# Two turns of a gather ring per iteration of VectorE's loop, in seven passes over the edges of a graph

## The chip, the cores and the metric

The kernel runs on one core of one Trainium2 chip. The metric is the device time of one execution, in microseconds. Three executions of the kernel before took 12166.11, 12187.51 and 12193.12 us; their median is 12187.51 us. Less is better.

## The reference

Four graph networks follow one another on one graph with 6250 nodes of 256 features and 100000 edges, sorted by destination. All of them gather the row of an edge's source node and sum such rows by destination node:

```python
# L0 (two layers) and L3: attention. ex is the softmax weight of an edge and head
out = segment_sum(h[src] * alpha[:, :, None], dst, N)
# L1: three graph convolutions
agg = segment_sum(x[src], dst, N); h = elu(agg @ W_rel + b + x @ W_root)
# L2: batch norm network
agg = segment_sum(edge_weight[:, None] * x[src], dst, N)
```

After each network a residual is added and a layer norm taken. So there are seven passes over the edges: two of L0, three of L1, one of L2, one of L3.

## The kernel before

The edges are padded so that every chunk of 128 edges belongs to one tile of 128 destination nodes. There are NCH = 832 chunks. Eight chunks (U = 8) make a unit; a pass has 104 units. The gathered rows lie in a ring with four slots (SLOTS = 4), one unit per slot, so that the ring goes round 26 times in a pass. Four units are called a turn here.

`aggregate_phase` (line 687) is one such pass, called seven times: l0a, l0b and l3 with a weight for each head, l2a with one weight per edge, and l1a, l1b, l1c (called the convolution passes below) with none. In it five instruction streams run beside each other and meet at semaphores only:

- GpSimd (POOL) waits until the index of the next unit is ready and issues eight indirect DMAs (`Ring.gather`, line 681), each of which gathers 128 rows of 1 KB from DRAM into the slot.
- VectorE (DVE) does three things for each unit. `begin` (line 745) builds the member matrices, 128x1024, one instruction for eight chunks (line 750). `take` (line 753) waits for the eight gathers and scales the slot, 128x2048 (line 761 or 765); in the convolution passes it only passes on a semaphore (line 757). `add` (line 768) loads the eight accumulator offsets of the unit into registers (line 772) and adds eight sums out of PSUM into the accumulator (line 779), each after a wait for its matmul (line 777) and one for the add before it.
- TensorE (PE) multiplies the member matrix of a chunk by its rows (line 815). It waits for `begin` and `take` of the unit, and, before it writes over a PSUM bank, for the add of the chunk eight back.
- ScalarE (ACT) waits until TensorE has summed all of a slot and copies the index of the unit four further on (line 731), which frees the slot for GpSimd.

VectorE's stream is written so that `begin` and `take` of the next unit stand ahead of `add` of this one. The loop at line 791 has one turn in its body, four units written out, and runs 25 times (`units // SLOTS - 1`). The 26th turn is written out behind it (lines 797 to 803), since its last unit has no next one. In the loop the unit's number is worked out from the loop's register, and each add has one register instruction for its address (line 776) and one for its wait (line 779); in the written-out turn the numbers are constants.

Of the kernel before, what the change touches and what calls it, by code (L numbers as in the profile page):

```python
# [14 lines left out]
SP_, SC = 125, 800  # L15
U = 8
SLOTS = 4
BY_GATHER = 2
FAR = 2.0 ** 100
NCH = -(-(E // P + 1 + NT) // (U * SLOTS)) * U * SLOTS  # L20
EP = NCH * P
# [19 lines left out]
I32 = mybir.dt.int32  # L41
assert E == SP_ * SC and NCH % (U * SLOTS) == 0 and NCH * P >= E + NT * (P - 1)


class Steps:


    def __init__(self, eng, sem):
        self.eng, self.sem, self.n = eng, sem, 0
# [620 lines left out]
class Ring:  # L670


    def __init__(self, m):
        self.messages = m.sb("messages", [P, SLOTS, U, MSGW])
        self.index = m.sb("index", [P, SLOTS, U], I32)
        self.gathered = [m.sem(f"gathered{s}") for s in range(SLOTS)]

# [9 lines left out]
def aggregate_phase(nc, k, name, table, acc, scale, head_scale, softmax, width, started=None):  # L687

    with ExitStack() as ctx:
        m = Mem(nc, ctx, name)
        slots = started or Ring(m)
        ring, index, gathered = slots.messages, slots.index, slots.gathered
        member = m.sb("member", [P, 2, U, P])
        sums = [m.ps(f"sums{j}", [P, 512]) for j in range(U)]
        turn = m.sem("gather_turn")
        index_ready = m.sem("index_ready")
        set_up = m.sem("set_up")
        prepared = m.sem("prepared")  # L700
        member_made = m.sem("member_made")
        chunk_summed = m.sem("chunk_summed")
        chunk_added = m.sem("chunk_added")
        half_cleared = m.sem("half_cleared")
        block = ctx.enter_context(nc.Block())
        half = NTP * MSGW // 2
        assert head_scale == (started is not None)
        units = NCH // U

        @block.gpsimd  # L710
        def _(pool):
            if started:
                pool.memset(acc[:, half:], 0.0).then_inc(half_cleared, 1)
            with pool.Fori(1 if started else 0, units // SLOTS) as i:
                for s in range(SLOTS):
                    pool.wait_ge(index_ready, i * SLOTS + s + 1)
                    pool.sem_inc(turn, 1)
                    slots.gather(pool, table, s)

        @block.scalar  # L720
        def _(act):
            def fill(s, u, index_too):

                if softmax:
                    ins = act.copy(ring[:, s, :, MSG_P:MSG_P + H],
                                   by_chunk(k.numer)[:, bass.ds(u * U, U), :])
                if width > MSG_M:
                    ins = act.copy(ring[:, s, :, MSG_M:MSG_M + H],
                                   by_chunk(k.first_max)[:, bass.ds(u * U, U), :])
                if index_too:  # L730
                    ins = act.copy(index[:, s, :], k.src[:, bass.ds(u * U, U)])
                ins.then_inc(index_ready, 1)

            act.wait_ge(set_up, 1)
            for s in range(SLOTS):
                fill(s, s, not started)
            with act.Fori(1, units // SLOTS) as i:
                for s in range(SLOTS):

                    act.wait_ge(chunk_summed, i * (SLOTS * U) + (s + 1 - SLOTS) * U)  # L740
                    fill(s, i * SLOTS + s, True)

        @block.vector
        def _(dve):
            def begin(i, s):

                u = i * SLOTS + s
                dve.wait_ge(index_ready, u + 1)

                dve.tensor_tensor(member[:, s % 2], repeat_outer(k.iota[:], U),  # L750
                                  repeat_inner(k.local[:, bass.ds(u * U, U)], P), ALU.is_equal).then_inc(member_made, 1)

            def take(i, s):
                dve.wait_ge(gathered[s], i * (16 * U) + 16 * U)
                msgs = ring[:, s, :, 0:D]
                if scale is None:
                    dve.sem_inc(prepared, 1)
                elif head_scale:
                    heads = msgs.rearrange("p j (h f) -> p j h f", h=H)
                    weights = by_chunk(scale)[:, bass.ds((i * SLOTS + s) * U, U), :]  # L760
                    dve.tensor_tensor(heads, heads, weights.unsqueeze(3).to_broadcast([P, U, H, C]),
                                      ALU.mult).then_inc(prepared, 1)
                else:
                    u = i * SLOTS + s
                    dve.tensor_tensor(msgs, msgs, repeat_inner(scale[:, bass.ds(u * U, U)], D),
                                      ALU.mult).then_inc(prepared, 1)

            def add(i, s):


                u = i * SLOTS + s
                offs = nc.values_load_multi_w_load_instructions(
                    k.tile_off[0:1, bass.ds(u * U, U)], engines=(mybir.EngineType.DVE,),
                    min_val=0, max_val=(NT - 1) * MSGW, skip_runtime_bounds_check_because="made so")[1]
                for j in range(U):
                    dve.wait_ge(chunk_summed, u * U + (j + 1))
                    dve.wait_ge(chunk_added, u * U + (j + 1))
                    at = acc[:, bass.ds(offs[j], width)]
                    dve.tensor_tensor(at, at, sums[j][:, 0:width], ALU.add).then_inc(chunk_added, 1)  # L779

            dve.memset(ring[:, :, :, MSG_ONE], 1.0).then_inc(set_up, 1)
            begin(0, 0)
            if started:

                take(0, 0)
                dve.memset(acc[:, 0:half], 0.0).then_inc(chunk_added, 1)
                dve.wait_ge(half_cleared, 1)
            else:
                dve.memset(acc, 0.0).then_inc(chunk_added, 1)
                take(0, 0)  # L790
            with dve.Fori(0, units // SLOTS - 1) as i:
                for s in range(SLOTS):
                    following = (i + (s + 1) // SLOTS, (s + 1) % SLOTS)
                    begin(*following)
                    take(*following)
                    add(i, s)
            last = units // SLOTS - 1
            for s in range(SLOTS):
                following = (last, s + 1) if s + 1 < SLOTS else None
                if following:  # L800
                    begin(*following)
                    take(*following)
                add(last, s)

        @block.tensor
        def _(pe):
            def sum_unit(i, s, first):
                u = i * SLOTS + s
                pe.wait_ge(member_made, u + 1)
                pe.wait_ge(prepared, u + 1)  # L810
                for j in range(U):
                    if not first:

                        pe.wait_ge(chunk_added, u * U + (j + 2 - U))
                    pe.matmul(sums[j][:, 0:width], member[:, s % 2, j, :], ring[:, s, j, 0:width],  # L815
                              start=True, stop=True).then_inc(chunk_summed, 1)

            for s in range(SLOTS):
                sum_unit(0, s, s == 0)
            with pe.Fori(1, units // SLOTS) as i:  # L820
                for s in range(SLOTS):
                    sum_unit(i, s, False)
# [102 lines left out]
def lookup_phase(nc, k, name, codes_dram, att_dram, z, z_self):  # L925
# [7 lines left out]
    NS = H * NT  # L933
    LP = U - BY_GATHER
    with ExitStack() as ctx:
# [8 lines left out]
        src_member = m.sb("src_member", [P, 2, 2, LP * P], BF16)  # L944
        index = m.sb("index", [P, SLOTS, BY_GATHER], I32)
        rows = m.sb("rows", [P, SLOTS, BY_GATHER, 2 * H])
        picked = m.sb("picked", [P, 2, LP, H])
# [32 lines left out]
        def _(act):  # L980
            def fill(s, u):
                act.copy(index[:, s, :], k.att_row[:, bass.ds(u * U + LP, BY_GATHER)]).then_inc(index_ready, 1)

# [8 lines left out]
        def _(pool):  # L992
            pool.wait_ge(att_stored, 16)
            with pool.Fori(0, units // SLOTS) as i:
                for s in range(SLOTS):
                    pool.wait_ge(index_ready, i * SLOTS + s + 1)
                    pool.sem_inc(turn, 1)
                    for j in range(BY_GATHER):
                        pool.indirect_dma_start(
# [5 lines left out]
        def _(dve):  # L1005
# [22 lines left out]
            def pick(i, r):  # L1028
# [9 lines left out]
                if z_self is not None:  # L1038
                    zs = by_chunk(z_self)[:, bass.ds(u * U, U), :]
                    dve.tensor_tensor(zs, dst[:, :, 0:H], dst[:, :, H:], ALU.add)  # L1040
                dve.wait_ge(gathered[r], i * (16 * BY_GATHER) + 16 * BY_GATHER)
                dve.tensor_tensor(by_chunk(z)[:, bass.ds(u * U + LP, BY_GATHER), :], rows[:, r, :, 0:H],
# [887 lines left out]
```

## Time and profile before

| what | value |
|---|---|
| executions, us | 12166.11, 12187.51, 12193.12 |
| the profiled execution, us | 12139.19 |
| its span, first to last instruction, us | 12137.7 |
| busy PE / PEld / DVE / ACT / POOL, us | 6937.7 / 4270.1 / 6291.8 / 691.5 / 7475.9 |
| mean granted TensorE clock | 0.678 |
| instructions in the profile | 120576 |

The page's busy times are sums over the whole span. No engine is busy for more than 62% of it (POOL), since the seven passes and the phases between them have different limits. The chain that the page follows back from the last instruction covers only the last layer norm and says nothing of the passes. So the passes are read one by one, by windows in time.

### The profile page before, as it was taken

To read this page: it belongs to the slowest core of one execution; us is meant where nothing else is said; L and a number is where in the kernel's file an instruction comes from. 1 tells how busy PE (TensorE), PEld (TensorE's weight loads), DVE (VectorE), ACT (ScalarE), POOL (GpSimd) and SP (SyncE) were. 2 spreads that over 40 slices of the span, in tenths; PEclk is the share of its full clock that TensorE was granted. 3 is DMA by queue.
4 is the path that set the end of the run, shared out by engine and by line. 5 is a ranking of instruction groups with operands and counts; after the bars stand their busy time and mean duration, and the time that the engine had idled before them with its cause. 6 is when DMAs were issued, how large, how long until landed. Compare 5 with 4: busy or idle time off the path is not lost. (4 is left out here: it accounts for less than half of the span.)

```text
span 12137.7 us, 120576 instructions
## 1 busy us (share of the span) xinstructions
PE 6937.7 (57%) x25379; PEld 4270.1 (35%) x25380; DVE 6291.8 (52%) x11430; ACT 691.5 (6%) x2515; POOL 7475.9 (62%) x6875
## 2 busy tenths in 40 slices
PE   1994544498545525556555565555545567965553
PEld 1443333343333312224322242233433344433332
DVE  5556555555655563344433343344655565555556
ACT  0001000100000000001100020000100012000000
POOL 0337777534777766665666646665577732357775
PEclk8556777655777756667766676667777775556776
DMA  2542333553233343333333333333333335533334
GB/s 90 131 111 75 87 88 88 135 121 104 74 88 87 87 107 88 90 88 91 90 89 87 88 92 88 89 89 87 104 88 88 88 78 154 121 83 87 88 88 101
DMA packets 574611, 1153.38 MB, mean 95 GB/s; under 512 B 141672, under 2 KB 335002, under 8 KB 573645
## 3 DMA queue, kind: packets, MB, share of 16 engines
q0 software_dynamic: 314480, 807.51, 25.1%
q1 hardware_dynamic: 253577, 338.53, 10.2%
q10 hardware_dynamic: 6480, 6.55, 0.2%
q8 instruction: 23, 0.38, 0.0%
q14 instruction: 51, 0.41, 0.0%
HBM read 1080.25 MB, written 78.23 MB: 95 GB/s over the span
## 5 line engine op out<-in xcount | busy, mean ns | idle before, releaser
L681 POOL DMA_INDIRECT l0bg_messages<-table_h,l0bg_index x832 | 1026.0, 1233 | 279.9 <-issue 253.0
L681 POOL DMA_INDIRECT l0ag_messages<-table_h,l0ag_index x832 | 1023.3, 1230 | 279.8 <-issue 253.0
L681 POOL DMA_INDIRECT l3g_messages<-table_h,l3g_index x832 | 1018.3, 1224 | 279.1 <-issue 253.0
L681 POOL DMA_INDIRECT l2a_messages<-table,l2a_index x832 | 985.4, 1184 | 291.2 <-issue 253.3
L681 POOL DMA_INDIRECT l1aa_messages<-table,l1aa_index x832 | 835.1, 1004 | 438.2 <-issue 248.4
L681 POOL DMA_INDIRECT l1ba_messages<-table,l1ba_index x832 | 833.2, 1001 | 409.1 <-issue 250.4
L681 POOL DMA_INDIRECT l1ca_messages<-table,l1ca_index x832 | 833.0, 1001 | 403.5 <-issue 246.1
L815 PE MATMUL l1aa_sums<-l1aa_messages,l1aa_member 128*128 128x256 f32 x1664 | 662.1, 532 | 724.4 <-issue 328.0
L815 PE MATMUL l2a_sums<-l2a_messages,l2a_member 128*128 128x257 f32 x1664 | 617.0, 549 | 672.9 <-DVE l_acc L779 567.1
L815 PE MATMUL l1ba_sums<-l1ba_messages,l1ba_member 128*128 128x256 f32 x1664 | 653.0, 524 | 607.0 <-issue 294.5
L815 PE MATMUL l1ca_sums<-l1ca_messages,l1ca_member 128*128 128x256 f32 x1664 | 660.2, 530 | 593.9 <-issue 316.1
L815 PE MATMUL l3a_sums<-l3g_messages,l3a_member 128*128 128x261 f32 x1664 | 636.3, 561 | 607.3 <-DVE l_acc L779 551.2
L815 PE MATMUL l0ba_sums<-l0bg_messages,l0ba_member 128*128 128x265 f32 x1664 | 633.4, 557 | 604.2 <-DVE l0b_acc L779 547.3
L815 PE MATMUL l0aa_sums<-l0ag_messages,l0aa_member 128*128 128x265 f32 x1664 | 615.3, 545 | 619.7 <-DVE l0a_acc L779 551.4
L815 PEld LDWEIGHTS l2a_sums<-l2a_messages,l2a_member 128*128 128x128 f32 x1664 | 466.2, 288 | 823.7 <-DVE l_acc L779 584.8
L815 PEld LDWEIGHTS l3a_sums<-l3g_messages,l3a_member 128*128 128x128 f32 x1664 | 470.2, 291 | 773.3 <-DVE l_acc L779 585.5
L815 PEld LDWEIGHTS l0ba_sums<-l0bg_messages,l0ba_member 128*128 128x128 f32 x1664 | 461.2, 286 | 776.2 <-DVE l0b_acc L779 582.8
L815 PEld LDWEIGHTS l0aa_sums<-l0ag_messages,l0aa_member 128*128 128x128 f32 x1664 | 450.1, 279 | 784.6 <-DVE l0a_acc L779 585.0
L815 PEld LDWEIGHTS l1aa_sums<-l1aa_messages,l1aa_member 128*128 128x128 f32 x1664 | 357.3, 248 | 1029.2 <-issue 642.5
L779 DVE TENSOR_TENSOR l1b_acc<-l1b_acc,l1ba_sums 128x256 f32 x832 | 350.4, 421 | 709.2 <-issue 404.0
L779 DVE TENSOR_TENSOR l1c_acc<-l1c_acc,l1ca_sums 128x256 f32 x832 | 350.4, 421 | 704.8 <-issue 415.2
L779 DVE TENSOR_TENSOR l1a_acc<-l1a_acc,l1aa_sums 128x256 f32 x832 | 350.4, 421 | 691.8 <-issue 402.3
(522 smaller groups left out, 12590.3 us busy)
## 6 DMA issues: line engine op xcount, KB each, us to landing
l0al_src_codes<-codes_dram SPq DMA_DIRECT2D x104, 384.0 KB
l0bl_src_codes<-codes_dram SPq DMA_DIRECT2D x104, 384.0 KB
l3l_src_codes<-codes_dram SPq DMA_DIRECT2D x104, 384.0 KB
l0al_dst_codes<-codes_dram SPq DMA_DIRECT2D x104, 256.0 KB
l0bl_dst_codes<-codes_dram SPq DMA_DIRECT2D x104, 256.0 KB
l3l_dst_codes<-codes_dram SPq DMA_DIRECT2D x104, 256.0 KB
l0ag_messages<-table_h,l0ag_index POOLq DMA_INDIRECT x832
l0bg_messages<-table_h,l0bg_index POOLq DMA_INDIRECT x832
```

The costliest lines, as they stand in the source:

```text
L681: pool.indirect_dma_start(out=self.messages[:, s, j, 0:D], out_offset=None, in_=table, in_offset=bass.IndirectOffsetOnAxis(ap=self.index[: ...
L779: dve.tensor_tensor(at, at, sums[j][:, 0:width], ALU.add).then_inc(chunk_added, 1)
L815: pe.matmul(sums[j][:, 0:width], member[:, s % 2, j, :], ring[:, s, j, 0:width], start=True, stop=True).then_inc(chunk_summed, 1)
```

## The change

A constant ROUNDS = 2 is added. VectorE's loop body holds ROUNDS turns, eight units, and the loop runs 12 times. Since the 25 turns that were in the loop are an odd number, one more turn is written out behind it, ahead of the one that was there. The order of the work, its instructions on tensors and the other engines' loops are as they were.

```diff
@@ -15,6 +15,7 @@
 SP_, SC = 125, 800
 U = 8
 SLOTS = 4
+ROUNDS = 2
 BY_GATHER = 2
@@ -788,13 +789,20 @@
             else:
                 dve.memset(acc, 0.0).then_inc(chunk_added, 1)
                 take(0, 0)
-            with dve.Fori(0, units // SLOTS - 1) as i:
-                for s in range(SLOTS):
-                    following = (i + (s + 1) // SLOTS, (s + 1) % SLOTS)
+            last = units // SLOTS - 1
+            assert last % ROUNDS == 1
+            with dve.Fori(0, last // ROUNDS) as i:
+                for n in range(ROUNDS * SLOTS):
+                    turn_now, turn_next = n // SLOTS, (n + 1) // SLOTS
+                    following = (i * ROUNDS + turn_next, (n + 1) % SLOTS)
                     begin(*following)
                     take(*following)
-                    add(i, s)
-            last = units // SLOTS - 1
+                    add(i * ROUNDS + turn_now, n % SLOTS)
+            for s in range(SLOTS):
+                following = (last - 1 + (s + 1) // SLOTS, (s + 1) % SLOTS)
+                begin(*following)
+                take(*following)
+                add(last - 1, s)
             for s in range(SLOTS):
                 following = (last, s + 1) if s + 1 < SLOTS else None
                 if following:
```

## Rows read from the trace of the kernel before

**Rows 1.** Groups by line, whole span: busy us, mean ns, idle before, what ended it

```profile
L681 POOL DMA_INDIRECT l0ag_messages<-table_h,l0ag_index x832 | 1023.3, 1230 | 279.8 <-issue 253.0 <-ACT l0ag_index L1161 20.1 <-ACT l0ag_index L731 6.6
...
L779 DVE TENSOR_TENSOR l0a_acc<-l0a_acc,l0aa_sums 128x265 f32 x832 | 357.8, 430 | 146.1 <-DVE l0a_acc L779 88.5 <-PE l0aa_sums L815 37.5 <-issue 20.2
...
L779 DVE TENSOR_TENSOR l1a_acc<-l1a_acc,l1aa_sums 128x256 f32 x832 | 350.4, 421 | 691.8 <-issue 402.3 <-PE l1aa_sums L815 146.1 <-DMA table<-l0b_acc 80.9
...
L761 DVE TENSOR_TENSOR l0ag_messages<-l0ag_messages,k_numer 128x2048 f32<-128x2048 f32 x104 | 238.4, 2292 | 366.1 <-DMA l0ag_messages<-table_h,l0ag_index 366.1
```

**Rows 2.** Busy us by engine in passes l0a, l1a and l2a

```profile
core 0: us, PE busy (x) PEld busy (x) DVE busy (x) ACT busy (x) POOL busy (x), PEclk, DMA share, GB/s
1018.00:2236.00 1218.00, 608.71 (x1648) 445.25 (x1648) 701.24 (x1037) 48.34 (x297) 954.04 (x800) 0.74 0.32 86
...
4478.00:5693.00 1215.00, 656.46 (x1648) 352.94 (x1648) 467.02 (x934) 19.53 (x99) 815.11 (x814) 0.67 0.33 88
...
8641.00:9872.00 1231.00, 611.74 (x1648) 462.14 (x1648) 694.03 (x1036) 19.52 (x99) 963.05 (x814) 0.71 0.32 87
```

**Rows 3.** What POOL waited for in steady l0a: us, times, longest

```profile
POOL l0ag_messages L681 <- issue: 224.0, 735, 0.3
```

**Rows 4.** The same for the three convolution passes

```profile
POOL l1ba_messages L681 <- ACT l1ba_index L731: 158.7, 35, 9.2
POOL l1ca_messages L681 <- ACT l1ca_index L731: 157.4, 34, 9.0
POOL l1aa_messages L681 <- ACT l1aa_index L731: 136.1, 40, 8.1
```

**Rows 5.** Timeline over a jump back, pass l0a: start, us, instruction, idle before

```profile
1422.70 0.43 DVE L779 TENSOR_TENSOR l0a_acc<-l0a_acc,l0aa_sums 128x265 f32 x1 [0.20 <-PE l0aa_sums L815]
...
1423.32 1.22 DVE L750 TENSOR_TENSOR l0aa_member<-k_iota,k_local 128x1024 f32<-128x1024 f32 x1 [0.19 <-issue]
...
1427.36 2.29 DVE L761 TENSOR_TENSOR l0ag_messages<-l0ag_messages,k_numer 128x2048 f32<-128x2048 f32 x1 [2.81 <-DMA l0ag_messages<-table_h,l0ag_index]
...
1434.31 1.22 DVE L750 TENSOR_TENSOR l0aa_member<-k_iota,k_local 128x1024 f32<-128x1024 f32 x1
```

**Rows 6.** VectorE's line 791, whole span: count, ns min/median/max

```profile
L791 DVEq FUSED_REGOPS  x175: 3/63/708, 1010.2 to 11960.1; - x175
L791 DVEq ALU_OP  x175: 1/40/701, 1047.4 to 12009.1; - x175
L791 DVEq COMPARE_BRANCH  x175: 2/56/710, 1047.5 to 12009.2; - x175
```

**Rows 7.** VectorE's address and wait instructions of the adds, whole span

```profile
L776 DVEq ALU_OP  x5600: 1/40/1400, 1011.4 to 12008.5; - x194
...
L777 DVEq EVENT_SEMAPHORE  x5824: 1/21/1402, 1015.5 to 12053.7; - x195
```

**Rows 8.** Line 776 in stretches of l0a, then l1a: ns min/median/max

```profile
L776 DVEq ALU_OP  x728: 40/40/40, 1105.9 to 2189.4; - x182
...
L776 DVEq ALU_OP  x685: 1/40/1400, 4601.1 to 5599.7; - x172
```

**Rows 9.** Timeline of VectorE over a jump back, pass l1a

```profile
4956.22 0.42 DVE L779 TENSOR_TENSOR l1a_acc<-l1a_acc,l1aa_sums 128x256 f32 x1 [1.71 <-PE l1aa_sums L815]
4959.64 1.23 DVE L750 TENSOR_TENSOR l1aa_member<-k_iota,k_local 128x1024 f32<-128x1024 f32 x1 [3.00 <-PE l1aa_sums L815]
4965.31 0.42 DVE L779 TENSOR_TENSOR l1a_acc<-l1a_acc,l1aa_sums 128x256 f32 x1 [4.45 <-issue]
```

**Rows 10.** DMA queues that carry instructions: packets, MB, share of 16 engines

```profile
q8 instruction: 23, 0.38, 0.0%
q14 instruction: 51, 0.41, 0.0%
```

**Rows 11.** Loads from DRAM by SyncE: count, KB each, median us to landing

```profile
l2b_xin<-table SPq DMA_DIRECT2D x100, 128.0 KB, 2.2
...
l3p_xin<-table SPq DMA_DIRECT2D x50, 128.0 KB, 2.8
```

## The prediction, made before the changed kernel ran

> **What bounds the kernel now.** I read the groups by line first, then windows of time over the seven passes, then who waits for whom in a steady stretch of each kind of pass, and last the timeline over a jump back. The groups [rows 1] put POOL's gathers at the top: 1023.3 us busy and 279.8 us idle in pass l0a, of which 253.0 us is its own issue time. The reader is to see that these two add up to 1303 us, more than the 1218 us from VectorE's loop on [rows 2], since the first gathers start ahead of it: POOL has no free time in that pass. [Rows 3] say the same of a steady stretch of 1100 us: POOL idles before 735 gathers for 0.3 us each and never for ScalarE, which frees the slots. VectorE waits there: 366.1 us in 104 waits for gathers to land, 3.5 us in each unit [rows 1]. So l0a is bound by the issue of gathers, and l0b, l2a and l3, which have the same instructions in VectorE's stream, are of its kind; [rows 2] show l2a with about the same POOL, DVE and PE sums.
>
> The convolution passes are another kind. Their 1215 us [rows 2] are as long, but POOL waits there for ScalarE's index, 136.1 to 158.7 us in each pass [rows 4]: now and then the ring is full, and what frees it is TensorE and VectorE. VectorE idles for 402.3 us before its adds with nothing that the profile names, against 20.2 us in l0a [rows 1]. The reason is in its sequencer: the register instruction at line 776 takes 40 ns always in l0a and up to 1400 ns in l1a [rows 8]. At a jump back that falls in such a slow stretch VectorE idles 3.00 us before the member instruction and 4.45 us before the next add [rows 9]; in l0a the jump costs 0.19 us [rows 5].
>
> **The change part by part.** *Fewer jumps back.* The loop is left or repeated 175 times now, 25 in each pass [rows 6], and 12 times in each after. Twelve of the 25 ends of a turn vanish inside an iteration and one more with the turn that is written out: 13 in each pass, with three instructions each. In the four scaled passes one costs 0.19 us of idle time [rows 5], against none at the member instruction inside a turn, at 1434.31. That is 4 x 13 x 0.19 = 10 us of VectorE's time. What hides it is the wait behind it: the scaling at 1427.36 waits 2.81 us for its gather [rows 5]. I take 0; if that cover were gone it would be a gain of 10 us.
>
> *A turn written out.* It has no address instruction for its adds: line 776 ran 5600 times, 7 x 25 x 32, and line 777 5824 times, 7 x 26 x 32 [rows 7]. Counted along VectorE's stream, a turn of a convolution pass in the loop is 156 instructions: 128 for 32 adds (the add, lines 776 and 777 [rows 7], and its wait at line 779), 3 at line 791 [rows 6], and 25 for begin, take and the offsets. Written out it is 104. So a pass saves 52 instructions there and 12 x 3 = 36 in the loop, 88 out of 25 x 156 = 3900. I expect the register arithmetic inside the body to stay as it is, one instruction for one sum of a multiple of the loop register and a constant.
>
> *What 88 instructions are worth in a convolution pass.* At the least nothing, or less than nothing if the body's arithmetic grows. From the nearest rows: VectorE idles 402.3 - 20.2 = 382 us more by issue in l1a than in l0a [rows 1], over 3900 instructions 0.098 us each, so 88 are 8.6 us and three passes 26 us of VectorE's time. The far end is that the whole pass goes by the count: 88 / 3900 = 2.3% of 1215 us, 27 us in each, 82 us in three. How much is seen at the end? POOL stands still for the ring in 136.1 of 1215 us, 0.11 [rows 2, 4]; the rest of the time it issues at its own pace, whatever VectorE does. I take 26 x 0.11 = 3 us, as POOL's share is the measured one, and keep 82 us for the range.
>
> *Added code.* Seven passes get a turn in the body and a turn behind it. They are loaded once, ahead of their use, beside gathers that leave the 16 DMA engines two thirds idle (DMA share 0.32 [rows 2]); I take 0. If a load isn't there in time, VectorE stands for one; the nearest rows are loads of 128 KB, which land after 2.2 to 2.8 us [rows 11].
>
> *What it doesn't touch.* No tensor instruction, DMA, wait or queue order moves, and no wait is added. The lead of begin and take over add is the same at each unit. In the sum: 12139.19 us of the profiled execution, less 3, is 12136 us; the median of the runs stands 48 us above that execution, so I forecast 12187.5 - 3 = 12184 us.
>
> **The rivals.** *A (slower): the body no longer stays loaded.* Place: the jump back, now over twice the code, in each iteration. For it speaks that VectorE's body grows from about 160 to about 315 instructions. Against it: all code that is loaded in 12137.7 us is 23 and 51 packets of 0.38 and 0.41 MB [rows 10], so with 175 loop ends [rows 6] nothing is loaded again now, and half of a body may well stay. Price: one load, 2.7 us with [rows 11], at 11 jumps back in a pass. In the scaled passes it is hidden by the 2.81 us at the same place [rows 5], and a delay of a few us beyond it by POOL, which never waits for a slot [rows 3]. In the convolution passes 3 x 11 x 2.7 = 89 us, all of it if the slow stretches make VectorE the limit, 10 us by POOL's share. Halfway that is 12184 + 50 = 12234 us. It decides from the point where VectorE has no wait behind the jump that covers the load: in the scaled passes above 2.81 us [rows 5], in a slow stretch at once. The Trainium skill, Runtime: NRT & Kernel Launch, section Instruction fetch mechanics, speaks for this rival: an engine other than TensorE keeps 32 KiB, 512 instructions, refilled in blocks of 16 KiB, and a taken branch to code outside the two blocks held forces a DMA fetch before the engine goes on. By its 64 bytes per instruction (32 KiB over 512) the body goes from 10 to 20 KiB, within the size but over more blocks. The trace differs from the page in one thing, that its 51 packets average 8 KB and not 16 [rows 10]; with pieces of 8 KB a body of 315 instructions lies in three or in four of them, depending on where each pass begins, so that I would expect some passes to be hit and others not. Read so, the page would give a third to two thirds of the 89 us.
>
> *B (faster): the convolution passes are VectorE's.* If its sequencer sets their time in the slow stretches, they shorten with the count of its instructions: between 26 and 82 us, halfway 54, 12187.5 - 54 = 12133 us. For it: [rows 8, 9], and POOL's waits for the ring. Against: POOL busy and issuing makes up most of the 1215 us.
>
> *C: the change doesn't do what it says.* The unit's number becomes i x 2 plus a turn; if each use took one more register instruction (8 for the address bases of a turn, say), the saving of 36 in the loop would be outweighed by 25 x 8 = 200 more, 164 net, less the 52: 112 x 0.098 x 3 = 33 us of VectorE's time and 4 us at the end: no change.
>
> **How the numbers follow.** 0.2%, 24 us, is about what a measurement of this kernel can tell from no change; its three runs lie 27 us apart. My forecast, with C in it, has 0.50: 12184 us, its own range 12160 to 12208. A has 0.27 and B 0.23. Part of A and B would stay within 24 us by POOL's share, and chance differences in the uneven convolution passes go both ways; they balance. So faster 0.22, same 0.50, slower 0.28. The range goes down to B's middle, 12133, a little less for the spread, and up to three quarters of A's price, 12184 + 67: 12130 to 12250 us.
>
> **What would show it.** Right: line 791's branch 84 times and not 175, line 776 5376 times (two written-out turns in each pass), VectorE's adds, members and scalings as many as before; scaled passes within 2 us of their windows; POOL in l0a still without a wait for ScalarE; in the convolution passes POOL's waits for the index within 20 us of [rows 4]. Rival A would show packets that carry instructions by the hundred, where code loaded once adds some tens to the 74 of [rows 10], and an idle stretch of 2 to 4 us before the member instruction at each jump back, also in l0a, where it would cost nothing. Rival B would show convolution passes of 1190 us, with less idle by issue before the adds. I am wrong if a scaled pass changes by more than 5 us, or the whole by more than 24 us.

## The result: slower by 0.23%, and the profile after

The changed kernel takes 12211.48 us (median of 17 runs, 12191.76 to 12236.85), the kernel before 12186.8 us (17 runs on the same chip, 12157.74 to 12198.3). The ratio is 1.0023, 95% interval 1.0016 to 1.0031: 25 us slower, a difference that can be told from none. The time lies in the range, but the forecast was no change.

One thing to know before traces are compared: the profiled execution before took 12139.19 us, less than any of its 17 timed ones, while that of the changed kernel (12212.48 us) is close to its median. So the traces differ by 73.3 us where the medians differ by 25: 35.8 us in the scaled passes, 24.9 in the convolution passes, 12.6 outside them.

The profiled execution of the changed kernel has a span of 12211.0 us and 119972 instructions. First the groups by line, as in [rows 1]:

```profile
L682 POOL DMA_INDIRECT l0ag_messages<-table_h,l0ag_index x832 | 1017.6, 1223 | 279.6 <-issue 252.8 <-ACT l0ag_index L1169 20.1 <-ACT l0ag_index L732 6.6
L780 DVE TENSOR_TENSOR l0a_acc<-l0a_acc,l0aa_sums 128x265 f32 x832 | 358.4, 431 | 150.5 <-DVE l0a_acc L780 90.5 <-PE l0aa_sums L823 43.0 <-issue 17.0
L780 DVE TENSOR_TENSOR l1a_acc<-l1a_acc,l1aa_sums 128x256 f32 x832 | 350.7, 421 | 713.1 <-issue 401.0 <-PE l1aa_sums L823 173.3 <-DMA table<-l0b_acc 74.4
...
L762 DVE TENSOR_TENSOR l0ag_messages<-l0ag_messages,k_numer 128x2048 f32<-128x2048 f32 x104 | 238.3, 2291 | 334.8 <-DMA l0ag_messages<-table_h,l0ag_index 334.6 <-issue 0.2
```

Then the queues that carry instructions, as in [rows 10]:

```profile
q14 instruction: 229, 1.88, 0.1%
q8 instruction: 23, 0.38, 0.0%
```

The 229 packets of instructions where there were 51 stand out. The mean of l0a's gathers seems to have gone down, 1223 ns against 1230 [rows 1], but that is the work of the first 32, which are issued ahead of VectorE's loop: they took 54.0 us and not 68.0. The other 800 took 963.6 us and not 955.3. Line by line the instructions came out as counted, against [rows 6, 7] (count, ns min/median/max, first and last start):

```profile
L794 DVEq COMPARE_BRANCH  x84: 1/56/710, 1096.6 to 12033.7; - x84
...
L777 DVEq ALU_OP  x5376: 1/40/1409, 1019.3 to 12033.0; - x200
...
L778 DVEq EVENT_SEMAPHORE  x5824: 1/21/1423, 1023.3 to 12127.9; - x195
```

The windows of l0a, l1a and l2a, laid by hand about as in [rows 2], are 8, 10 and 19 us wider (the table below measures the passes from instruction to instruction):

```profile
core 0: us, PE busy (x) PEld busy (x) DVE busy (x) ACT busy (x) POOL busy (x), PEclk, DMA share, GB/s
1026.00:2252.00 1226.00, 622.51 (x1648) 454.08 (x1648) 699.65 (x1037) 48.34 (x297) 962.11 (x800) 0.72 0.32 86
4486.00:5711.00 1225.00, 665.31 (x1648) 353.88 (x1648) 469.42 (x920) 19.72 (x100) 831.20 (x827) 0.67 0.33 88
8660.00:9910.00 1250.00, 609.78 (x1632) 460.42 (x1632) 697.03 (x1016) 20.21 (x104) 992.30 (x829) 0.70 0.32 87
```

In l0a POOL gained busy time over the same 800 instructions, 962.11 against 954.04 us [rows 2]: 8 us, as much as the window. VectorE's is 1.6 us less. TensorE's rose too, by 14 us at a granted clock of 0.72 against 0.74, but it isn't what the pass waits for: in the first experiment below TensorE was busy for 625.58 us in l0a, and the pass was as short as before. What POOL waited for did not change (as in [rows 3, 4]: us, times, longest):

```profile
POOL l0ag_messages L682 <- issue: 222.7, 731, 0.3
...
POOL l1ba_messages L682 <- ACT l1ba_index L732: 157.2, 36, 9.0
POOL l1ca_messages L682 <- ACT l1ca_index L732: 152.9, 41, 9.0
```

So POOL has no more idle time, its gathers last longer. A table worked out from the traces shows it for all seven passes (first member instruction to last add, us; stretch is the time by which POOL's gathers of 92 steady units, the 11th to the 102nd, exceed 0.949 us each):

| pass | before | after | stretch before | after |
|---|---|---|---|---|
| l0a | 1230.9 | 1239.1 | 178.5 | 186.5 |
| l0b | 1232.8 | 1240.6 | 180.9 | 189.9 |
| l2a | 1259.4 | 1269.6 | 173.7 | 184.5 |
| l3 | 1228.5 | 1238.1 | 178.1 | 187.5 |
| l1a, l1b, l1c | 1241.1, 1253.6, 1248.1 | 1249.2, 1262.6, 1255.9 | 36 to 38 | 39 to 44 |

Each scaled pass is 8 to 10 us longer, 36 us in all, and its gathers are stretched by 8 to 11 us more. The passes repeat well: with one turn per iteration, or with its effect given back (two experiments below), other executions had 4944.6 and 4947.2 us in the four together, against 4951.6 here; with the change, and its code shifted so that none is loaded again, one had 4991.0 against 4987.4. The convolution passes don't repeat so well, see below. Where the stretch comes from is seen in the start distance of POOL's units of eight gathers. Before, in l0a, they took 12.2, 12.2, 12.2 and 11.3 us in a turn; the short one is that in which VectorE jumps back. After, l0b, l2a and l3 have seven of 12.1 to 12.3 and one of 11.4 in every two turns. Half of the short units are gone, 0.84 us each, with the jump.

Here is why a unit at a jump back is short. POOL and VectorE in l0a of the kernel before, from a unit without a jump to one with it; the member instruction behind the jump is the one at 1423.32 in [rows 5]:

```profile
1410.95 1.22 DVE L750 TENSOR_TENSOR l0aa_member<-k_iota,k_local 128x1024 f32<-128x1024 f32 x1
1411.17 1.82 POOL L681 DMA_INDIRECT l0ag_messages<-table_h,l0ag_index  x1 [0.30 <-issue]
...
1413.29 0.95 POOL L681 DMA_INDIRECT l0ag_messages<-table_h,l0ag_index  x1 [0.30 <-issue]
...
1416.09 2.29 DVE L761 TENSOR_TENSOR l0ag_messages<-l0ag_messages,k_numer 128x2048 f32<-128x2048 f32 x1 [3.92 <-DMA l0ag_messages<-table_h,l0ag_index]
1417.05 2.15 POOL L681 DMA_INDIRECT l0ag_messages<-table_h,l0ag_index  x1 [0.30 <-issue]
...
1423.26 0.94 POOL L681 DMA_INDIRECT l0ag_messages<-table_h,l0ag_index  x1 [0.30 <-issue]
...
1424.51 0.96 POOL L681 DMA_INDIRECT l0ag_messages<-table_h,l0ag_index  x1 [0.30 <-issue]
```

A gather issue lasts 0.95 us and starts every 1.25 us. One that starts while the member instruction runs (1411.17, inside 1410.95 to 1412.17) lasts 1.82 us: it ends at 1412.99, 0.82 us after the member instruction. One that starts inside a scaling lasts 2.15 us: it ends at 1419.20, 0.82 us after the scaling's end at 1418.38. In each unit one gather meets the member instruction and one the scaling. At the jump back the member instruction came 0.19 us later [rows 5]. It started just after one gather (1423.26) and ended just as the next started (1424.51), and neither was stretched: 1.82 - 0.95 = 0.87 us saved, on POOL, which sets the pace. In the changed kernel, between the two turns of a body:

```profile
1433.22 0.95 POOL L682 DMA_INDIRECT l0ag_messages<-table_h,l0ag_index  x1 [0.30 <-issue]
...
1434.29 1.22 DVE L751 TENSOR_TENSOR l0aa_member<-k_iota,k_local 128x1024 f32<-128x1024 f32 x1
1434.47 1.85 POOL L682 DMA_INDIRECT l0ag_messages<-table_h,l0ag_index  x1 [0.30 <-issue]
```

No idle time ahead of the member instruction, and the gather that starts 0.18 us into it is stretched to 1.85 us. Twelve or thirteen ends of a turn went in a pass: 12 x 0.84 = 10 us. This is my theory (the collision theory). A count over the 92 steady units bears it out: before, a member instruction stretched a gather in 70 of them in each scaled pass, after in 80 or 81, and a scaling stretched one in all 92 both times. The Trainium skill, SBUF — State Buffer, section Who interferes with whom, names such a rule: a VectorE instruction with two SBUF inputs shares a read interface with GpSimd instructions that read SBUF, and the one that comes second waits. The section doesn't say that an indirect DMA is such an instruction, and it tells of a probe in which tensor_tensor did not stall a DMA. The trace agrees with the rule for the gather that comes second, with 0.82 us beyond the end of VectorE's instruction, and not with that probe. The trace doesn't agree for the other order: the member instruction at 1423.32, which starts 0.06 us after a gather, lasts its 1.22 us. The prediction didn't weigh this rule.

### The profile page after: what moved, and what is told of

Its sections match the earlier page's. It is cut to its first block and busy times, and to the rows that moved or that the text cites. A ratio compares the mean times of both kernels' runs of the same rounds, so it can differ in the third digit from the quotient of the medians.

```text
span 12211.0 us, 119972 instructions
## 1 busy us (share of the span) xinstructions
PE 6972.4 (57%) x25379; PEld 4295.7 (35%) x25380; DVE 6291.6 (52%) x11430; ACT 691.1 (6%) x2515; POOL 7498.1 (61%) x6875
## 3 DMA queue, kind: packets, MB, share of 16 engines
q14 instruction: 229, 1.88, 0.1%
## 5 line engine op out<-in xcount | busy, mean ns | idle before, releaser
L682 POOL DMA_INDIRECT l0ag_messages<-table_h,l0ag_index x832 | 1017.6, 1223 | 279.6 <-issue 252.8
```

Source lines behind the costliest of these rows:

```text
L682: pool.indirect_dma_start(out=self.messages[:, s, j, 0:D], out_offset=None, in_=table, in_offset=bass.IndirectOffsetOnAxis(ap=self.index[: ...
```

## The experiments

**Giving the short pause back.** Only where the changed kernel has no jump back any more, the member instruction waits for the last add ahead of it:

```diff
-            def begin(i, s):
+            def begin(i, s, pause=False):
                 u = i * SLOTS + s
+                if pause and not (isinstance(u, int) and u < 1):
+                    dve.wait_ge(chunk_added, (u - 1) * U + 1)
                 dve.wait_ge(index_ready, u + 1)
...
-                    begin(*following)
+                    begin(*following, pause=n == SLOTS)
...
-                    begin(*following)
+                    begin(*following, pause=s == 0)
```

> The changed kernel with one thing added: VectorE waits for its last add ahead of the member instruction at the places where a jump back used to stand (the middle of an iteration, and between the two written-out turns). Theory 1, the pause: in the scaled passes of the changed kernel a unit of gathers takes 12.2 us where no jump stands and 11.35 us where one does, since the short idle time ahead of the member instruction lets a gather's issue begin before it; with 12 such places fewer a scaled pass loses about 10 us. By it this kernel has the short units back, the scaled passes are 8 to 10 us shorter each than with the change, and the time is about 12211 - 40 = 12171 to 12187 us. Rival, reloading: the three passes l0a, l1b, l1c whose jump takes 3 to 4 us cost the time; they still do here, so 12211 us stays.

Measured: 12168.58 us (11 runs, 12152.9 to 12177.1), ratio 0.9986 (0.9976 to 0.9996) against the kernel before (12181.08 us, 34 runs on the same chip, which are those of the next three experiments too). The scaled passes are 1229.2, 1231.1, 1258.8 and 1228.1 us, all within 2 us of those before. The trace at the same place:

```profile
1426.33 0.95 POOL L682 DMA_INDIRECT l0ag_messages<-table_h,l0ag_index  x1 [0.30 <-issue]
1426.44 1.23 DVE L753 TENSOR_TENSOR l0aa_member<-k_iota,k_local 128x1024 f32<-128x1024 f32 x1 [0.24 <-DVE l0a_acc L782]
1427.59 0.96 POOL L682 DMA_INDIRECT l0ag_messages<-table_h,l0ag_index  x1 [0.30 <-issue]
```

A pause of 0.24 us, no stretched gather. An added wait takes back the whole loss in the scaled passes, while code is loaded as without it (229 packets here too) and a pass has one instruction more in the trace, not fewer. So it is the pause and not the loading.

**A pause ahead of every member instruction**, in the kernel before:

```diff
-            def begin(i, s):
+            def begin(i, s, pause=True):
                 u = i * SLOTS + s
+                if pause and not (isinstance(u, int) and u < 1):
+                    dve.wait_ge(chunk_added, (u - 1) * U + 1)
                 dve.wait_ge(index_ready, u + 1)
```

> The kernel before (one turn per iteration) with VectorE waiting for its last add ahead of every member instruction, in all passes. By the pause theory the other three units of each turn become 11.35 us as well: 4 scaled passes x 26 turns x 3 units x 0.84 us = 262 us less, 11925 us; the member instruction then falls between two issues of gathers, and the stretched issues per unit go from two to one. If the pause must be as long as the jump's (0.3 us) and a wait for the add gives too little, nothing changes: 12187 us. By the reloading theory nothing changes either. In the convolution passes the wait costs or gives a few us either way.

Measured: 12179.8 us (12 runs), ratio 0.9999 (0.9985 to 1.0013). The collisions get fewer, as expected: POOL's stretch in l0a falls from 178 to 112 us. But the passes don't follow, and of the 262 us that I expected little is seen in the scaled passes and nothing in all: l0a takes 1217.6 us, 13 less, and the convolution passes grow by 16 to 46 us each (by the traces). VectorE's adds in l0a now idle by issue as they did only in the convolution passes:

```profile
L781 DVE TENSOR_TENSOR l0a_acc<-l0a_acc,l0aa_sums 128x265 f32 x832 | 357.8, 430 | 360.0 <-issue 145.0 <-PE l0aa_sums L817 121.3 <-DVE l0a_acc L781 60.5
```

145.0 us against 20.2 us [rows 1]. And POOL, which never waited for ScalarE in the steady stretch of l0a [rows 3], waits 54.4 us for it here. A second limit stands close behind the first: VectorE's sequencer, as I read the idle time by issue.

**Is it loading of code (rival A)?** Two kernels shift the changed kernel's code with waits that are already satisfied, so that no body is loaded again, or all seven are. Two such lines make one instruction: 121 and 127 instructions in all ahead of the loops, and 116 and 49 more in a branch of the sorting that isn't taken here (the first kernel's numbers are shown):

```diff
+PADS = dict(zip(('l0aa', 'l0ba', 'l1aa', 'l1ba', 'l1ca', 'l2a', 'l3a'), (0, 0, 38, 36, 36, 82, 50)))
...
+            for _ in range(232 if not high else 0):
+                dve.wait_ge(base_ps_made, 1)
...
             dve.memset(ring[:, :, :, MSG_ONE], 1.0).then_inc(set_up, 1)
+            for _ in range(PADS[name]):
+                dve.wait_ge(set_up, 1)
             begin(0, 0)
```

> The changed kernel, its code shifted (instructions put where they aren't run, and 121 satisfied waits ahead of five of the passes, about 8 us in all) so that by the instructions' places no pass has a body that lies in four pieces of 8 KB. Reloading theory: no jump takes 3 to 4 us, the packets of code fall from 229 to about 66, and the time goes back to 12187 + 8 us. Pause theory: the jumps become short, but the time stays at 12211 + 8 us, since a reload is hidden by the wait for the gathers.

> The same with other shifts (127 satisfied waits): by the places all seven bodies lie in four pieces, so that all seven passes reload at each jump. Reloading theory: seven passes pay and not three, 25 x 7 / 3 = 58 us over the kernel before, 12245 + 8 us, and more where a conv pass is hit. Pause theory: as e3, 12219 us; scaled passes are no longer than with the change although their jumps take 4 us; code packets above 450.

Measured, on one chip: 12216.4 us (10 runs), ratio 1.0034 (1.0023 to 1.0045), without reload; 12205.58 us (11 runs), ratio 1.0019 (1.001 to 1.0028), with a reload at every jump. From the branch to the next member instruction it took 0.53 to 0.58 us (medians) in all passes of the one, 3.4 to 3.8 us in those of the other. The packets on the queue of instructions, first without reload:

```profile
q14 instruction: 66, 0.54, 0.0%
```

Then with a reload everywhere:

```profile
q14 instruction: 451, 3.69, 0.1%
```

In the changed kernel itself l0a, l1b and l1c are hit (4.0, 3.2 and 3.1 us), the other four passes aren't (l0b 0.57 us). A jump of l0a in it:

```profile
1485.83 1.23 DVE L751 TENSOR_TENSOR l0aa_member<-k_iota,k_local 128x1024 f32<-128x1024 f32 x1 [3.69 <-issue]
```

VectorE stood 77 times for 3 us (11 jumps in each of seven passes), and it cost nothing: the kernel with all of them is if anything the faster. Rival A falls. By the traces a reload isn't without effect on the scaled passes: without reload they take 1238.9, 1240.6, 1271.0 and 1240.5 us (l0a, l0b, l2a, l3), with it 1243.4, 1232.6, 1263.0 and 1231.6 us. That is 4 us more in l0a and 8 to 9 us less in each of the others. By the collision theory a stand of 3 us, too, moves the instructions that follow it against the gathers; I didn't follow it gather by gather. What a jump back is worth is not the same at either length.

**What do instructions cost in VectorE's stream?** In the kernel before, four more satisfied waits ahead of each member instruction, 16 per turn:

```diff
             def begin(i, s):
                 u = i * SLOTS + s
+                for _ in range(8):
+                    dve.wait_ge(set_up, 1)
                 dve.wait_ge(index_ready, u + 1)
```

(Eight such lines make four instructions: the profile has 123663 in place of 120576, 3087 more for 728 units, 4.2 in each.)

> The kernel before with four more sequencer instructions in each unit on VectorE (satisfied waits ahead of the member instruction, 16 more in a turn, on some 156 to 160). Theory, a cap: over tens of us VectorE's sequencer passes no more than about 3.3 instructions per us (156 in 47 us in the convolution passes, where 402 us of idle time have no named cause; in the run with a pause ahead of every member instruction such idle time came up in the scaled passes too, once they would have run faster). By it a turn takes 172/3.3 = 52 us: convolution passes 1250 + 26 x 4.8 = 1375 us, scaled passes up to 100 us more each, the whole about 12181 + 700. Rival, no cap: 4 x 0.07 us per unit are hidden by the wait for gathers in the scaled passes, 12181 to 12210 us.

Measured: 12257.76 us (4 runs) against 12138.49 us (17 runs on the same chip, those of the next three experiments too), ratio 1.0112 (1.0089 to 1.0136). The convolution passes grow by 40 to 67 us (1302.7, 1293.8, 1314.7), 16 x 25 = 400 instructions in each, so 0.14 us per instruction in the mean. The scaled passes shrink to 1216.5, 1210.8, 1253.8 and 1203.6 us: to them the four waits are a pause ahead of each member instruction, and the stretch falls to 130 to 138 us. My expectation, a hard limit on instructions per time and 700 us more in all, was several times too high.

**One wait per unit** instead of eight, in the kernel before. `add` waits once for the last of TensorE's eight sums; the second kernel of this pair has the pause ahead of every member instruction as well:

```diff
+                dve.wait_ge(chunk_summed, u * U + U)
                 for j in range(U):
-                    dve.wait_ge(chunk_summed, u * U + (j + 1))
                     dve.wait_ge(chunk_added, u * U + (j + 1))
```

> The kernel before with VectorE waiting once per unit for all its matmuls and not once per add: about 28 instructions fewer in a turn (132 and not 160; 128 and not 156). Cap: the convolution passes, 47 us per turn, go down to POOL's own pace, 8 x 1.254 us and one stretched issue per unit, about 43 us per turn: 1150 us and not 1250, in all 12181 - 300 = 11880 us; the scaled passes, bound by POOL, stay (or change by where the member instruction falls against the issues of gathers). No cap: the convolution passes stay at 1250 us or get longer, since an add waits for the whole unit: 12181 to 12250 us.

> The last one with the wait for the last add ahead of every member instruction. If both the pause and the cap are as I think, the scaled passes have the room now that they lacked with the pause alone: units of 11.3 us and not 12.17, four passes of 1230 - 60 us, and the convolution passes as in the run with one wait: 12181 - 300 - 250 = 11630 us. If the pause gives nothing by itself, as the last run.

Measured: 12005.57 us (4 runs), ratio 0.9888 (0.9873 to 0.9903), for one wait; 12103.79 us (7 runs), ratio 0.9974 (0.9963 to 0.9985), for one wait and a pause ahead of each member instruction. My limit said 300 us less for one wait; it was 133. The pause, which helped above, costs 98 us here, 0.8%. The traces of the two tell why; the kernel with one wait at a jump back and a unit later:

```profile
1417.21 1.22 DVE L750 TENSOR_TENSOR l0aa_member<-k_iota,k_local 128x1024 f32<-128x1024 f32 x1 [0.19 <-issue]
1417.62 1.64 POOL L681 DMA_INDIRECT l0ag_messages<-table_h,l0ag_index  x1 [0.30 <-issue]
...
1428.87 1.22 DVE L750 TENSOR_TENSOR l0aa_member<-k_iota,k_local 128x1024 f32<-128x1024 f32 x1
1429.55 1.35 POOL L681 DMA_INDIRECT l0ag_messages<-table_h,l0ag_index  x1 [0.30 <-issue]
```

and the one with the pause:

```profile
1428.24 1.23 DVE L752 TENSOR_TENSOR l0aa_member<-k_iota,k_local 128x1024 f32<-128x1024 f32 x1 [0.29 <-DVE l0a_acc L781]
1428.56 1.73 POOL L681 DMA_INDIRECT l0ag_messages<-table_h,l0ag_index  x1 [0.30 <-issue]
```

With one wait the 832 adds of l0a idle for 98.8 us in all and not 146.1 [rows 1], and end earlier against the gathers. The next gather starts 0.68 us into the member instruction and is held only until 0.81 us after its end, 1.35 us in all. A later member instruction (0.41 us ahead of the gather at the jump, 0.32 us with the pause) holds it for 1.64 and 1.73 us. So a pause is neither good nor bad: what counts is at what point of the member instruction the next gather starts, and the time is (member's end + 0.82) - gather's start, at least 0.95. I had expected the pause to help again; the same rule, read rightly, gives the loss: by the traces l0a's gathers are stretched by 187 us with the pause against 160 without, and the pass takes 1240.7 us against 1210.7.

In the convolution passes one wait takes the idle time by issue from 402.3 us [rows 1] to 41.5:

```profile
L779 DVE TENSOR_TENSOR l1a_acc<-l1a_acc,l1aa_sums 128x256 f32 x832 | 350.9, 422 | 721.9 <-DMA table<-l0b_acc 446.8 <-ACT l1aa_index L731 110.2 <-issue 41.5
```

but the sum of idle time stays at 721.9 (691.8 before): the wait moved to the gathers, the only DMAs that VectorE waits for in a pass (the profile puts the name of another, `table<-l0b_acc`, on it). By the traces those passes win 12 to 26 us each, and the scaled ones 16 to 22 us.

**The two-turn body in the convolution passes alone**, one turn in the scaled ones:

```diff
-            with dve.Fori(0, last // ROUNDS) as i:
+            rounds = ROUNDS if scale is None else 1
+            with dve.Fori(0, last // rounds) as i:
...
-            for s in range(SLOTS):
+            for s in range(SLOTS if last % rounds else 0):
```

> The change in the three convolution passes alone; the four scaled passes keep one turn per iteration. By the pause theory the loss is all in the scaled passes, so this one has the gain of the 88 fewer instructions per convolution pass and none of the loss: as the run with the pauses put back, 12169 us, ratio 0.9986. Rival, the loss is in the convolution passes (unit times there are uneven, and their jumps reload code): 12195 to 12211 us.

Measured: 12111.85 us (11 runs), ratio 0.9977 (0.9968 to 0.9986) against 12138.49 us: 27 us faster. The scaled passes are those of before again (1228.7, 1229.7, 1258.6, 1227.6 us). This splits the change: a gain of 20 to 27 us in the convolution passes (27 us by the times, of which 7 us lie in the scaled passes by the traces), and the whole of the loss in the scaled ones, 36 us by the traces (the two ratios differ by 0.0046, 56 us, by their far ends 37 to 77).

**Taking the collision away.** In the four scaled passes the member instruction covers 128x8 instead of 128x1024, in the kernel before and in the changed one. The members are zero there, so these two kernels leave out the sums of the scaled passes; the gathers, scalings, matmuls and adds are all issued:

```diff
+                if scale is None:
                     dve.tensor_tensor(member[:, s % 2], repeat_outer(k.iota[:], U),
...
+                else:
+                    dve.tensor_tensor(member[:, s % 2, 0, 0:U], k.iota[:, 0:U],
+                                      k.local[:, bass.ds(u * U, U)], ALU.is_equal).then_inc(member_made, 1)
...
+            if scale is not None:
+                dve.memset(member[:], 0.0).then_inc(set_up, 1)
+                dve.wait_ge(set_up, 2)
```

> The kernel before, where in the four scaled passes the member instruction covers 128x8 instead of 128x1024 (the members are zero there, so the sums of these passes are left out); the scalings stay. Collision theory: the 1.22-us member instruction no longer lies over the start of a gather, so each unit's stretch of one gather from 0.95 to 1.82 us goes: units of 11.3 us instead of 12.17, and the short unit at the jump back is no shorter than the others. POOL's stretch in a scaled pass falls from 178 us to about 100, the passes from 1230 to 1155-1180 us, the whole to 11870-11950 us. Rival (the jump back itself gives time, by the sequencer or by code): three long units and a short one of 0.8 us less stay, whatever the member's length.

> The same 128x8 member instruction in the scaled passes of the changed kernel. Collision theory: with nothing to collide, it matters no longer how many jumps back there are: the scaled passes are within 2 us of those of the kernel before with the same edit, where the changed kernel was 8 to 10 us slower in each; the conv passes keep their gain of 15 to 27 us, so this kernel is 15 to 30 us faster than its partner. Rival: it stays 8 to 10 us slower in each scaled pass, and so some 15 us slower in all.

Measured: 12220.93 us, ratio 1.0018 (1.0006 to 1.003), and 12235.75 us, ratio 1.0035 (1.002 to 1.0049), 12 runs each against 12190.61 us. The mechanism came out, the time didn't. No gather is stretched by the member instruction any more (from the first of the two):

```profile
1158.00 0.16 DVE L754 TENSOR_TENSOR l0aa_member<-k_iota,k_local 128x8 f32<-128x8 f32 x1
...
1158.19 0.94 POOL L681 DMA_INDIRECT l0ag_messages<-table_h,l0ag_index  x1 [0.31 <-issue]
1158.50 2.29 DVE L765 TENSOR_TENSOR l0ag_messages<-l0ag_messages,k_numer 128x2048 f32<-128x2048 f32 x1 [0.34 <-DMA l0ag_messages<-table_h,l0ag_index]
...
1159.44 2.18 POOL L681 DMA_INDIRECT l0ag_messages<-table_h,l0ag_index  x1 [0.30 <-issue]
```

The stretch in l0a falls from 178 to 119 us, about what the scalings make (92 x 1.25 = 115), and no unit is short by its place in the turn: the median unit of l0a takes 11.2 to 11.4 us at every place, the 11.3 us of the collision theory, where its rival said that three long units and a short one stay. But the pass is as long as before, 1231.7 us, for the other limit takes over. Its group by line:

```profile
L783 DVE TENSOR_TENSOR l0a_acc<-l0a_acc,l0aa_sums 128x265 f32 x832 | 358.5, 431 | 388.3 <-issue 164.6 <-PE l0aa_sums L822 91.1 <-DVE l0a_acc L783 67.7
```

And what POOL waited for in l0a from 1100 to 2200 us, as in [rows 3]:

```profile
POOL l0ag_messages L681 <- issue: 224.4, 723, 3.8
POOL l0ag_messages L681 <- ACT l0ag_index L731: 61.3, 10, 9.3
```

The adds idle 164.6 us by issue, the ring fills and POOL waits 61.3 us for the index in the steady stretch where it never waited [rows 3]. Between the two kernels the scaled passes (in the order l0a, l0b, l2a, l3) differ by +12.1, +5.1, +4.2 and -2.5 us, 19 in all and uneven, where I expected 2 at most and the rival 8 to 10 in each. The whole is 15 us slower, as the rival had it, and not 15 to 30 us faster, as I had; but the two intervals overlap. Since POOL now waits, and no longer sets all of their time, this pair doesn't measure the jump's worth. It is inconclusive on that, and clear on the stretch.

**The change on top of one wait**: both diffs of one wait and of the two-turn body together, with the body in the convolution passes alone, then in all:

> One wait for TensorE's last matmul of a unit in place of eight, and the two-turn body in the convolution passes alone. If what is left of the convolution passes with one wait (1228 us, their adds waiting for DMAs and not by issue) is POOL's, fewer instructions of VectorE bring nothing more: 12005 us within 12. If VectorE's count still tells there, 27 us less: 11980 us.

> One wait per unit, and the two-turn body in all seven passes. With one wait the scaled passes have units of 11.67 to 12.03 us with no short one at the jump back, so if only the phase of the member instruction against the gathers' starts matters, the jumps have no fixed price here: within 15 us of the kernel with one wait and one turn, either sign. If a jump back is worth 0.84 us whatever the timing, it is 40 us slower: 12045 us.

Measured against 12190.61 us: 12064.93 us (4 runs), ratio 0.9892 (0.9875 to 0.9909), and 12041.51 us (4 runs), ratio 0.9873 (0.9857 to 0.989). With one wait and no change of the loop the ratio was 0.9888 on another chip. Neither of the two can be told from that, as I expected of both (a fixed price of 0.84 us for each jump would have made the second 40 us slower), and all three beat both kernels of the case by 1.1 to 1.3%. Between themselves the two do differ: on one chip all four runs of the second (12027.42 to 12043.21 us) are below all four of the first (12058.5 to 12069.32), by 23 us in the medians. In the scaled passes the two-turn body is now faster: 1205.8, 1207.6, 1236.8 and 1208.6 us against 1211.1, 1211.9, 1240.3 and 1212.0 in the kernel that has it only in the convolution passes, 3.4 to 5.3 us each, 16 to 17 us of the 23. That is the rule once more with the other sign. Here a jump back makes the held gather 1.64 us instead of 1.35, and 12 x 0.29 = 3.5 us go with the jumps.

## Why the prediction was wrong

- The step that failed is "fewer jumps back": 0.19 us of idle time in each, hidden behind the scaling's wait, "I take 0; if that cover were gone it would be a gain of 10 us". The size was right and so was the cover on VectorE. What the step left out is what the 0.19 us did to another engine: it moved a VectorE instruction off the start of a gather. Each short jump back that goes costs POOL 0.84 us: 8 to 10 us in each scaled pass, 36 us in all. The pause put back took that away; the loading of code, switched off and on, did not.
- I wrote that a scaled pass is bound by POOL's issue and left VectorE out of its time. The first half holds. The second took the gathers' busy time as fixed, though [rows 1] gave 1230 ns as the mean of an instruction that lasts 950 ns where nothing meets it. No step of the prediction asked where the 280 ns are from: they were 1023.3 - 832 x 0.95 = 233 us in l0a alone, 178 of them in the steady units.
- The signs that I set, scaled passes within 2 us if right and more than 5 us if wrong, were the right test: they moved by 8 to 10. That the total, 25 us, is so close to my limit of 24 us says little: a loss of 36 us and a gain of some 11 meet in it.
- The convolution passes: I took 3 us of a possible 26. The change in them alone brought 27 us (17 to 39). The counted price (0.098 us per instruction; the added waits gave 0.14) was of the right size, the factor 0.11 for POOL's share was too small by several times: of the 26 us of VectorE's time 10 to 27 were seen. The profiled execution of the changed kernel has them 25 us longer and not shorter than that before. These passes differ by as much and more between executions (3725 to 3776 us for the three together in six traces of kernels with the two-turn body there and a wait per add), and the profiled execution before was a quick one; from the profile alone this part could not be judged.
- Rival A was right on the place and the mark (l0a, l1b and l1c load code again at each jump, 178 packets more than before) and wrong on the price, which is nothing. Its idle stretch in l0a, 3.69 us ahead of a member instruction, cost that pass nothing, as said: 1239.1 us with it, 1238.9 without reload. Rival B's mechanism is there with a fifth to a half of its price, and the loss in the scaled passes outweighs it. C didn't happen: the branch ran 84 times, the address instruction 5376 times, the profile has 604 instructions less, 7 x 88 = 616 by my count.
- POOL's waits for the index stayed within 5 us of [rows 4] in all three convolution passes, as said (l1a 137.0 us from 4486 to 5711 us).

The sum by what was measured: +36 us in the scaled passes, some 10 to 27 us less in the others, so +9 to +26; the timed difference is +25.

## What to carry to other kernels

When one engine sets the pace, don't take its mean instruction time as given: compare its shortest with its mean, and look in the timeline at what runs on the other engines when a long one starts. An idle gap that is hidden on its own engine can still be worth something, or cost something, by where it puts the next instruction against those of the engine that is the bound. In such a kernel an edit's sign can turn with the phase, as it did here twice, and so an edit that gave nothing or lost is worth another look after the next one.

## What the runs showed of the hardware

- A DMA_INDIRECT on POOL that starts inside a VectorE TENSOR_TENSOR with both inputs in SBUF is held until 0.82 us after that instruction's end (means over 92 gathers in l0a before: 2.23 us inside a scaling, against 0.948 for the 552 that start beside both). In the 14 traces of this case 12887 gathers (of 92 steady units in each pass) start inside a member instruction of 128x1024 or a scaling; all but 244 follow (end + 0.82) - start, at least 0.945, to within 0.02 us. The 244 start less than 0.05 us after VectorE's instruction does, and aren't held at all. One that starts inside an add, whose second input is in PSUM, is not: 276 gathers in l0a of the kernel with one wait, 0.945 us in the mean.
- The Trainium skill, Runtime: NRT & Kernel Launch, section Instruction fetch mechanics, has code in two blocks of 16 KiB, and a fetch for a jump out of them. The trace agrees that a jump back to code that isn't held makes VectorE stand, for 3.1 to 4.0 us from the branch to the next member instruction. Its packets are of 8.2 KB (1.88 MB in 229), so half of such a block or a smaller piece, which isn't settled; there are five per jump ((451 - 66) / 77 with a reload at each of 77 jumps, (229 - 66) / 33 in the changed kernel).
- VectorE's sequencer has a slow stretch, in which register and wait instructions that take 20 to 40 ns take up to 1.4 us [rows 7, 8]. It is not a matter of the pass: it appeared in l0a when its gathers were less stretched (idle by issue 20.2 us before, 145.0 and 164.6 us in two experiments), and with seven waits fewer in a unit it was nearly gone (41.5 us in l1a against 402.3). What starts it wasn't settled, nor whether an execution that isn't profiled has it.
